# Attention scores from 50-row stacks of six bf16 products, with the heads in the two halves of TensorE's array

## The chip, the core and the metric

The kernel runs on one core of one Trainium2 chip. The metric is the device time of one launch in microseconds (us); lower is better.

## The reference

One layer: attention with a residual and a layer norm, then a mixture of experts with a residual and a layer norm. The input is 8 batches of 512 tokens with 128 channels. What matters here is the attention:

```python
qkv = x @ w_qkv + b_qkv
qkv = qkv.reshape(B, N_HEADS, S, 3 * HEAD_DIM)          # 8, 16, 512, 24: a head is 32 tokens wide in the buffer
q, k, v = jnp.split(qkv, 3, axis=-1)                    # HEAD_DIM = 8
scores = jnp.einsum('bhqd,bhkd->bhqk', q, k) * scale    # 512 x 512 for each of 128 (batch, head)
attn = jax.nn.softmax(scores, axis=-1)
vals = jnp.einsum('bhqk,bhkd->bhqd', attn, v)
```

Everything is float32. A float32 value is the sum of three bf16 parts (high, middle, low), so a score over 8 channels can be made as one bf16 matmul whose contraction rows hold products of parts: the kernel stacks part pairs over the partitions.

## The kernel before

The attention runs over 32 quads (a quad is 128 tokens of x and gives four heads of 512 queries and keys), four quads to a batch of the input. Each engine has its own program, ordered by hand, and goes through the same stages. Stage q does several things at once, for different quads:

- step `at` = 0 to 7 of the stage takes one half of one head. TensorE (PE) makes the plain scores of quad q + 2 (`score_a`, two matmuls of 512 columns into one of two pairs of PSUM banks), from which VectorE (DVE) takes the maximum over the keys (line 916). It also makes the transposed scores of quad q (`score_b`, two matmuls, one PSUM bank each), with the maximum subtracted by two more stack rows, and ScalarE (ACT) takes their exponential (line 883). The PE order inside a step is A, B, A, B.
- after each odd step PE multiplies the exponentials of quad q - 1 with v (`pvp`, line 1006): four float32 matmuls, one in each 32-column group.
- between steps there are jobs through one PSUM bank, `shared`: xT (the transpose of x, step 4), qkv (the projection, step 6), mT (the transpose of the maxima, step 1), valsT (the transpose of the output, step 3), and once a batch proj (i = 2, step 0), oT (i = 1, step 7), x1T (i = 3, step 5), gate (i = 3, step 7) and counts (i = 1, step 2). Here i is q modulo 4.

Two waits couple the engines inside a stage. The first matmul of `score_a` in a step waits for the maximum of two steps ago. A matmul of `score_b` waits for the exponential that last read its bank, the one of the same c in the step before.

The stacks are made as follows. After the qkv job of stage q - 1 (that is of quad q + 3) ACT copies q and k to SBUF, GpSimd (POOL) splits them into three bf16 parts (lines 810 to 816), SyncE's (SP) queue writes the parts to DRAM (line 742), waits for that write, and then reads them back as stack rows (lines 753 and 757). Stage q + 1 may begin on PE only when that stack is in. SP also loads x, the residual input (line 765), the experts' weights in stages 0 to 4, and stores the layer norm's output (line 644). POOL clears a buffer in DRAM in stages -1 to 7 (line 797) and later scatters rows into it.

In the kernel before a stack has 72 rows: nine products of parts by 8 channels (`KR = 9 * HD`), and 74 with the maximum's two rows. All four heads of a quad use the same partitions, one after the other in the free dimension.

Of the kernel before, what the change touches and what calls it, by code (L numbers as in the profile page):

```python
# [45 lines left out]
P = 128  # L46
# [58 lines left out]
def layer(nc, x, w_qkv, b_qkv, w_out, b_out, wg, ws1, ws3, ws2, we1, we3, we2, out):  # L105
# [26 lines left out]
    with ctx:  # L132
        def sb(name, shape, dt=F32):
            return ctx.enter_context(nc.sbuf_tensor(name, shape, dt))
# [8 lines left out]
        parts_dram = nc.dram_tensor("parts_dram", (2, 2, 4, 3, P, 32), BF16).ap()  # L143
# [143 lines left out]
        def need(eng, s, value):  # L287
# [4 lines left out]
            if not isinstance(value, int) and eng.engine in ALONE:  # L292


                eng.sem_inc(passed, 1)

# [398 lines left out]
        def attention_sync(sp):  # L695
# [36 lines left out]
            def stage(b, i):  # L732
# [3 lines left out]
                if has(b, i, 3):  # L736
# [5 lines left out]
                    sp.dma_start(parts_dram[par].rearrange("k h i p t -> p (k h i) t"),  # L742
                                 parts[:].rearrange("p k h i t -> p (k h i) t")).then_inc(parts_stored, 16)
# [34 lines left out]
        def attention_gpsimd(pool):  # L778
# [21 lines left out]
            def stage(b, i):  # L800
# [3 lines left out]
                if has(b, i, 4):  # L804
# [5 lines left out]
                    pool.tensor_copy(parts[:, :, :, 0, :], qk32[:]).then_inc(split_step, 1)  # L810
                    need(pool, split_step, 3 * n + 1)
                    pool.tensor_tensor(qkr[:], qk32[:], parts[:, :, :, 0, :], ALU.subtract).then_inc(split_step, 1)
                    need(pool, split_step, 3 * n + 2)
                    pool.tensor_copy(parts[:, :, :, 1, :], qkr[:]).then_inc(split_step, 1)
                    need(pool, split_step, 3 * n + 3)
                    pool.tensor_tensor(parts[:, :, :, 2, :], qkr[:], parts[:, :, :, 1, :], ALU.subtract) \
# [761 lines left out]
```

## Time and profile before

| | us |
|---|---|
| median of 3 runs | 738.19 |
| fastest, slowest | 734.01, 744.85 |
| the profiled execution | 739.75 |
| span of its instructions | 738.00 |

The profiled execution took 1.75 us more than the span from its first to its last instruction. Attention fills the trace up to about 515 us, and the mixture of experts the rest. The mean granted TensorE clock over the span is 0.964.

### The profile page before, as it was taken

The numbers are of one execution on the slowest core, as the hardware profiler recorded it, in microseconds if no ns is written. First come the engines' busy times: TensorE is split into PE (matmuls) and PEld (weight loads), VectorE is DVE, ScalarE is ACT, GpSimd is POOL, SyncE is SP. The second block draws the span as 40 slices with busy tenths as digits, with TensorE's granted clock in tenths as the row PEclk, the third lists the DMA queues.
The fourth block names the chain that finished last, engine by engine and source line by source line (L and its number), as shares of the span: only waits on it lengthen the run. The fifth ranks groups of instructions, "written<-read, shape, count | busy, mean of one in ns | idle before, by whom it ended". The sixth has DMA issues, their size and how long they took to land.

```text
span 738.0 us, 16592 instructions
## 1 busy us (share of the span) xinstructions
PE 657.1 (89%) x4593; PEld 315.6 (43%) x4594; DVE 551.3 (75%) x1272; ACT 426.0 (58%) x973; POOL 268.9 (36%) x402
## 2 busy tenths in 40 slices
PE   1899999999999999999999999997979898887880
PEld 1232333333333433433333343332568676666660
DVE  4967777879979969987996997974566566765763
ACT  1056677667766757666775666666342354454552
POOL 3124114213342244143434224306053265555553
PEclk9999999999999999999999999999899999999985
DMA  4366675543244233333233323302320333343322
GB/s 79 72 147 138 150 142 109 112 110 78 54 95 92 52 75 81 68 85 79 54 62 82 93 54 72 73 2 58 100 59 22 82 84 98 93 139 108 100 73 71
DMA packets 161854, 62.65 MB, mean 85 GB/s; under 512 B 110586, under 2 KB 155516, under 8 KB 161808
## 3 DMA queue, kind: packets, MB, share of 16 engines
q1 hardware_dynamic: 152960, 46.46, 29.0%
q0 software_dynamic: 5648, 13.26, 5.9%
q10 hardware_dynamic: 3200, 2.36, 1.0%
q8 instruction: 23, 0.38, 0.2%
q14 instruction: 23, 0.19, 0.1%
HBM read 38.04 MB, written 24.26 MB: 84 GB/s over the span
## 4 chain that ended last, share of the span: by engine, by line
PE 78%; ACT 5%; issue 5%; DVE 5%; DMA 2%; another core or an unknown queue 2%; POOL 1%; SPq 1%; ACTq 0%; DVEq 0%; POOLq 0%
PE pvp L1006 17%; PE scoreB L986 16%; PE scoreA L972 15%; PE scoreB L1520 5%; ACT prob L883 3%; PE pvp L1507 2%; PE scoreA L1497 2%; PE scoreA L1499 2%; PE scoreA L1498 2%; PE shared L525 2%; PE shared L514 2%; PE scoreB L1447 1%; DVE mx L916 1%; PE shared L544 1%
## 5 line engine op out<-in xcount | busy, mean ns | idle before, releaser
L916 DVE TENSOR_REDUCE mx<-scoreA 128x2 f32<-128x1024 f32 x256 | 306.3, 1220 | 77.0 <-PE scoreA L972 74.1
L883 ACT ACTIVATE prob<-scoreB 128x512 f32<-128x512 f32 x512 | 279.8, 600 | 128.0 <-PE scoreB L986 122.4
L972 PE MATMUL scoreA<-ks,qs 72*128 72x512 bf16 x512 | 205.7, 409 | 12.6 <-DMA ks<-parts_dram 10.2
L986 PE MATMUL scoreB<-qs,ks 74*128 74x512 bf16 x512 | 200.5, 394 | 15.3 <-ACT prob L883 11.9
L1006 PE MATMUL pvp<-prob,v 128*32 128x512 f32 x1024 | 141.4, 626 | 0.8 <-ACT pv_sb L875 0.8
L972 PEld LDWEIGHTS scoreA<-ks,qs 72*128 72x128 bf16 x512 | 51.0, 102 | 156.1 <-DVE mx L916 65.5
L986 PEld LDWEIGHTS scoreB<-qs,ks 74*128 74x128 bf16 x512 | 49.8, 98 | 110.6 <-ACT prob L883 85.3
L1166 POOL DMA_INDIRECT y_dram<-prob x72 | 70.6, 981 | 71.3 <-ACT prob L1397 43.3
L810 POOL CAST parts<-qk 128x256 bf16<-128x256 f32 x32 | 12.7, 396 | 227.9 <-ACT v_raw L563 208.6
L488 POOL DMA_INDIRECT slots_dram<-rows,slot_i x64 | 63.3, 990 | 31.7 <-issue 17.4
L1397 ACT ACTIVATE prob<-scoreB,prob 128x128 f32<-128x128 f32 x72 | 26.5, 368 | 38.4 <-PE scoreB L1520 26.1
L1520 PE MATMUL scoreB<-w,prob 128*128 x288 | 47.1, 289 | 0.0
L1336 DVE TENSOR_TENSOR prob<-scoreA,prob 128x256 f32<-128x256 f32 x72 | 30.4, 422 | 22.0 <-ACT prob L1390 16.2
L1390 ACT ACTIVATE prob<-scoreA 128x256 f32<-128x256 f32 x72 | 27.6, 383 | 28.1 <-PE scoreA L1499 17.9
L1497 PE MATMUL scoreA<-w_high,ebT_high 128*128 x72 | 35.7, 496 | 8.2 <-DVE ebT_low L1271 5.2
L1520 PEld LDWEIGHTS scoreB<-w,prob 128*128 128x128 f32 x288 | 40.1, 201 | 0.5
L1507 PE MATMUL pvp<-ident,prob 128*128 128x128 f32 x144 | 29.6, 288 | 11.0 <-DVE prob L1341 9.6
L1271 DVE TENSOR_TENSOR ebT_low<-scoreA,ebT_high 128x128 fp32r<-128x128 f32 x72 | 20.7, 288 | 23.5 <-ACT ebT_high L1365 15.9
L1006 PEld LDWEIGHTS pvp<-prob,v 128*32 128x32 f32 x1024 | 20.6, 109 | 31.0 <-issue 29.4
L1341 DVE COPY prob<-pvp 128x256 f32<-128x256 f32 x72 | 29.8, 414 | 2.0 <-remote 1.2
L559 ACT ACTIVATE qk<-shared,bq 128x128 f32<-128x128 f32 x64 | 20.0, 363 | 17.8 <-PE shared L514 12.0
L1507 PEld LDWEIGHTS pvp<-ident,prob 128*128 128x128 f32 x144 | 16.5, 145 | 30.6 <-issue 19.9
(172 smaller groups left out, 880.4 us busy)
## 6 DMA issues: line engine op xcount, KB each, us to landing
qs<-parts_dram SPq DMA_DIRECT2D x96, 96.0 KB
parts_dram<-parts SPq DMA_DIRECT2D x32, 192.0 KB
slots_dram<-blank POOLq DMA_DIRECT2D x9, 520.0 KB
prob<-slots_dram SPq DMA_DIRECT2D x72, 65.0 KB
ks<-parts_dram SPq DMA_DIRECT2D x64, 64.0 KB
prob<-y_dram SPq DMA_DIRECT2D x8, 512.0 KB
ks<-parts_dram SPq DMA_DIRECT2D x32, 96.0 KB
xin<-in_L_attn_x SPq DMA_DIRECT2D x32, 64.0 KB, 2.0
```

The costliest lines, as they stand in the source:

```text
L488: pool.indirect_dma_start(slots_dram, bass.IndirectOffsetOnAxis(ap=slot_i[:, j, t:t + 1], axis=0), rows[:, t, j, :], None).then_inc(scatte ...
L883: act.activation(prob[:, i % 2, j, 2 * u + c, :], scoreB[:, c], ACT.Exp, scale=SCALE).then_inc(exp_done, 1)
L916: dve.tensor_reduce(mx[:, i % 2, at // 2, at % 2 * 2:at % 2 * 2 + 2], scoreA[:, at % 2], AX.X, ALU.max).then_inc(max_done, 1)
L972: ins = pe.matmul(scoreA[:, at % 2, c], qs[0:KR, st, j, qc * P:(qc + 1) * P], ks[0:KR, st, j, :], start=True, stop=True)
L986: pe.matmul(scoreB[:, c], ks[0:KM, i, j, kc * P:(kc + 1) * P], qs[0:KM, i, j, :], start=True, stop=True).then_inc(b_ready, 1)
L1006: ins = pe.matmul(pvp[32 * h:32 * h + 32, :], v[:, (i - 1) % 2, h, j, :], prob[:, (i - 1) % 2, h, j, :], start=(j == 0), stop=(j == 3))
L1166: pool.indirect_dma_start(y2_dram, bass.IndirectOffsetOnAxis(ap=eb[:, at, D:D + 1].bitcast(I32), axis=0), yo[:, r, :], None, bounds_check= ...
L1336: dve.tensor_tensor(gated[:, r % 2, :], scoreA[:, 0, r % 2, F:2 * F], silu[:, r % 2, :], ALU.mult) \
L1341: dve.tensor_copy(gatedT[:, (r - 1) % 2, :], pvp[:, 0:F]).then_inc(gT_copied, 1)
L1497: pe.matmul(h, ebT_high[:, r % 2, 0:P], high, start=True, stop=False)
L1507: ins = pe.transpose(pvp[:, c * P:(c + 1) * P], gated[:, (r - 1) % 2, c * P:(c + 1) * P], ident[:])
L1520: ins = pe.matmul(y, gatedT[:, r % 2, c * P:(c + 1) * P], w2_flat[:, bass.ds(e * NFC * D + c * D, D)], start=(c == 0), stop=(c == NFC - 1))
```

## The change

The three smallest of the nine products are left out (middle times low, low times middle, low times low), so a stack has 48 rows, and 50 with the maximum's two. Heads 0 and 2 of a quad lie in partitions 0 to 49, heads 1 and 3 in partitions 64 to 113. The matmuls of both score loops become tiles of 64 rows by 128 columns at row 0 or at row 64 of the array. `score_b` takes the heads in the order 1, 0, 3, 2 (`head_b`), so that in each step A and B lie in different halves. The buffers `parts`, `qs` and `ks` are laid out to fit. The split's four POOL instructions keep their sizes. The stack is read back with 12 transfers instead of 8, which together move two thirds of the bytes (each row of 512 tokens is 1 KB).

```diff
-    KR = 9 * HD
-    PR = 3 * HD
-
-    K_ROWS = [(0, 0, 3), (PR, 1, 3), (PR + 2 * HD, 0, 1), (2 * PR, 2, 3), (2 * PR + HD, 0, 2)]
-    STACK_DMAS = 3 + len(K_ROWS)
+    KR = 6 * HD
     KM = KR + 2
+    HALF = P // 2
+
+    PRODUCTS = ((0, 0, 3), (3 * HD, 0, 2), (5 * HD, 0, 1))
+    STACK_DMAS = 4 * len(PRODUCTS)
...
-        parts = sb("parts", [P, 2, 4, 3, 32], BF16)
-        qs = sb("qs", [P, 4, 4, 512], BF16)
-        ks = sb("ks", [P, 4, 4, 512], BF16)
+
+        parts = sb("parts", [P, 4, 6, 32], BF16)
+
+        qs = sb("qs", [P, 4, 2, 512], BF16)
+        ks = sb("ks", [P, 4, 2, 512], BF16)
...
+        def head_b(at):
+
+            return at // 2 ^ 1
+
...
-                    for r in range(3):
-                        sp.dma_start(qs[PR * r:PR * (r + 1), st],
-                                     parts_dram[par, 0].rearrange("h i (d c) t -> (i d) h (c t)", d=HD)) \
-                          .then_inc(stack_loaded[par], 16)
-                    for row, i0, i1 in K_ROWS:
-                        sp.dma_start(ks[row:row + HD * (i1 - i0), st],
-                                     parts_dram[par, 1, :, i0:i1].rearrange("h i (d c) t -> (i d) h (c t)", d=HD)) \
-                          .then_inc(stack_loaded[par], 16)
+                    for row, first, end in PRODUCTS:
+                        for half in range(2):
+                            at = HALF * half + row
+                            n_rows = HD * (end - first)
+                            for to, s0 in ((qs, first), (ks, 6 - end)):
+                                sp.dma_start(to[at:at + n_rows, st],
+                                             parts_dram[par, half::2, s0:s0 + end - first]
+                                             .rearrange("h s (d c) t -> (s d) h (c t)", d=HD)) \
+                                  .then_inc(stack_loaded[par], 16)
...
-                                act.activation(prob[:, i % 2, j, 2 * u + c, :], scoreB[:, c], ACT.Exp,
+                                act.activation(prob[:, i % 2, head_b(2 * j), 2 * u + c, :], scoreB[:, c], ACT.Exp,
...
-                                act.dma_start(qs[KR + m:KR + m + 1, (i + 1) % 4].rearrange("p h x -> p (h x)"),
+                                act.dma_start(qs[KR + m::HALF, (i + 1) % 4].rearrange("p h x -> p (h x)"),
...
-            dve.memset(ks[64:96, 0], 1.0).then_inc(ones_set, 1)
+            dve.memset(ks[:, 0], 1.0).then_inc(ones_set, 1)
...
-                        ins = pe.matmul(scoreA[:, at % 2, c], qs[0:KR, st, j, qc * P:(qc + 1) * P],
-                                        ks[0:KR, st, j, :], start=True, stop=True)
+                        row = HALF * (j % 2)
+                        ins = pe.matmul(scoreA[:, at % 2, c], qs[row:row + KR, st, j // 2, qc * P:(qc + 1) * P],
+                                        ks[row:row + KR, st, j // 2, :], start=True, stop=True)
...
-                        j, kc = at // 2, at % 2 * 2 + c
+                        j, kc = head_b(at), at % 2 * 2 + c
...
-                        pe.matmul(scoreB[:, c], ks[0:KM, i, j, kc * P:(kc + 1) * P], qs[0:KM, i, j, :],
-                                  start=True, stop=True).then_inc(b_ready, 1)
+                        row = HALF * (j % 2)
+                        pe.matmul(scoreB[:, c], ks[row:row + KM, i, j // 2, kc * P:(kc + 1) * P],
+                                  qs[row:row + KM, i, j // 2, :], start=True, stop=True).then_inc(b_ready, 1)
```

The instructions of PE, ACT, DVE and POOL keep their order and number. The one queue whose contents change is SP's. In the loop over batches, in the stage i = 0, from the write of the parts to the end of the stack's loads, SP's queue before holds these rows (the two REGISTER_ALU rows belong to a wait):

```order
L742 DMA parts_dram<-parts 128x24x32
L291 REGISTER_ALU x2
L753 DMA qs<-parts_dram 24x4x512 x3
L757 DMA ks<-parts_dram 24x4x512
L757 DMA ks<-parts_dram 16x4x512
L757 DMA ks<-parts_dram 8x4x512 x2
L757 DMA ks<-parts_dram 16x4x512
```

In the changed kernel SP's queue holds these rows in the same place, of which four are left out ahead of the last four:

```order
L748 DMA parts_dram<-parts 128x24x32
L293 REGISTER_ALU x2
L763 DMA qs<-parts_dram 24x2x512
L763 DMA ks<-parts_dram 24x2x512
L763 DMA qs<-parts_dram 24x2x512
L763 DMA ks<-parts_dram 24x2x512
...
L763 DMA qs<-parts_dram 8x2x512
L763 DMA ks<-parts_dram 8x2x512
L763 DMA qs<-parts_dram 8x2x512
L763 DMA ks<-parts_dram 8x2x512
```

Nothing moved past anything else; the loads went from 8 to 12, and each covers two heads instead of four.

## Rows read from the trace of the kernel before

**Rows 1.** The page: busy time of each engine, and the chain that ended last.

```profile
PE 657.1 (89%) x4593; PEld 315.6 (43%) x4594; DVE 551.3 (75%) x1272; ACT 426.0 (58%) x973; POOL 268.9 (36%) x402
...
PE 78%; ACT 5%; issue 5%; DVE 5%; DMA 2%; another core or an unknown queue 2%; POOL 1%; SPq 1%; ACTq 0%; DVEq 0%; POOLq 0%
```

**Rows 2.** Windows (us, then PE, PEld, DVE, ACT, POOL, granted clock): stage 4, then stages 16 to 19.

```profile
98.78:112.41 13.63, 13.56 (x107) 4.74 (x106) 10.43 (x12) 9.91 (x22) 3.32 (x7) 1.00 0.73 146
...
277.23:292.00 14.77, 14.04 (x108) 4.76 (x106) 13.49 (x29) 10.61 (x23) 5.95 (x9) 1.00 0.42 94
292.00:306.41 14.41, 14.35 (x113) 5.67 (x114) 13.14 (x30) 9.92 (x22) 5.39 (x11) 1.00 0.30 60
306.41:321.10 14.69, 14.66 (x116) 5.68 (x114) 13.84 (x32) 10.23 (x22) 3.64 (x7) 1.00 0.31 59
321.10:338.85 17.75, 16.41 (x118) 6.39 (x118) 11.46 (x16) 10.36 (x24) 7.17 (x11) 0.90 0.35 78
```

**Rows 3.** Waits from 68 to 470 us: waiter, releaser, total us, times, longest.

```profile
ACT prob L883 <- PE scoreB L986: 104.0, 94, 2.7
...
DVE mx L916 <- PE scoreA L972: 55.4, 73, 2.8
```

**Rows 4.** Timeline, PE and ACT, steps 0 and 1 of a stage: start, us.

```profile
319.92 0.39 PE L972 MATMUL scoreA<-ks,qs 72*128 72x512 bf16 x1
320.14 0.38 PE L986 MATMUL scoreB<-qs,ks 74*128 74x512 bf16 x1
...
320.62 2.16 ACT L883 ACTIVATE prob<-scoreB 128x512 f32<-128x512 f32 x4
...
321.76 0.39 PE L986 MATMUL scoreB<-qs,ks 74*128 74x512 bf16 x1
...
322.19 1.06 PE L1006 MATMUL pvp<-prob,v 128*32 128x512 f32 x8
323.19 0.39 PE L972 MATMUL scoreA<-ks,qs 72*128 72x512 bf16 x1
```

**Rows 5.** Timeline, PE, steps 6 and 7 of the stage before that.

```profile
316.13 0.39 PE L972 MATMUL scoreA<-ks,qs 72*128 72x512 bf16 x1
...
317.02 0.38 PE L509 MATMUL shared<-xT,wq 128*128 128x128 f32 x2
...
318.61 0.38 PE L986 MATMUL scoreB<-qs,ks 74*128 74x512 bf16 x1
318.92 1.06 PE L1006 MATMUL pvp<-prob,v 128*32 128x512 f32 x8
```

**Rows 6.** Timeline, SP's queue: stores of the parts and loads of stacks, three stages.

```profile
35.18 1.83 SPq L757 DMA_DIRECT2D ks<-parts_dram  x5
...
112.96 0.38 SPq L742 DMA_DIRECT2D parts_dram<-parts  x1
119.73 1.15 SPq L753 DMA_DIRECT2D qs<-parts_dram  x3
...
322.31 0.38 SPq L742 DMA_DIRECT2D parts_dram<-parts  x1
326.27 1.15 SPq L753 DMA_DIRECT2D qs<-parts_dram  x3
327.46 1.85 SPq L757 DMA_DIRECT2D ks<-parts_dram  x5
```

**Rows 7.** Timeline, PE at the start: the first matmul of stage 0, two later ones.

```profile
39.47 0.61 PE L972 MATMUL scoreA<-ks,qs 72*128 72x512 bf16 x1 [0.36 <-DMA ks<-parts_dram]
...
57.63 0.63 PE L972 MATMUL scoreA<-ks,qs 72*128 72x512 bf16 x1
58.06 0.63 PE L986 MATMUL scoreB<-qs,ks 74*128 74x512 bf16 x1
```

**Rows 8.** Timeline, a pause of PE in a stage i = 3; windows, late attention.

```profile
329.30 0.39 PE L986 MATMUL scoreB<-qs,ks 74*128 74x512 bf16 x1 [1.19 <-ACT prob L883]
...
490.00:508.00 18.00, 14.76 (x112) 4.03 (x105) 11.88 (x43) 12.81 (x26) 7.50 (x9) 1.00 0.07 21
```

More of the change, by code:

```diff
@@ L140, in sem @@
             return ctx.enter_context(nc.semaphore(name))
-        parts_dram = nc.dram_tensor("parts_dram", (2, 2, 4, 3, P, 32), BF16).ap()
+        parts_dram = nc.dram_tensor("parts_dram", (2, 4, 6, P, 32), BF16).ap()
         x1_dram = nc.dram_tensor("x1_dram", (TILES * P, D), F32).ap()
@@ L741, in stage @@
                     need(sp, stack_loaded[par], 16 * STACK_DMAS * (2 * b + (i + 3) // 2))
-                    sp.dma_start(parts_dram[par].rearrange("k h i p t -> p (k h i) t"),
-                                 parts[:].rearrange("p k h i t -> p (k h i) t")).then_inc(parts_stored, 16)
+                    sp.dma_start(parts_dram[par].rearrange("h s p t -> p (h s) t"),
+                                 parts[:].rearrange("p h s t -> p (h s) t")).then_inc(parts_stored, 16)
                     need(sp, parts_stored, 16 * (n + 1))
@@ L809, in stage @@
                     need(pool, split_done, n)
-                    pool.tensor_copy(parts[:, :, :, 0, :], qk32[:]).then_inc(split_step, 1)
+                    high, mid, low = parts[:, :, 0::5], parts[:, :, 1:5:3], parts[:, :, 2:4]
+                    full, rest = (t[:].rearrange("p k h t -> p h k t") for t in (qk32, qkr))
+                    pool.tensor_copy(high, full).then_inc(split_step, 1)
                     need(pool, split_step, 3 * n + 1)
-                    pool.tensor_tensor(qkr[:], qk32[:], parts[:, :, :, 0, :], ALU.subtract).then_inc(split_step, 1)
+                    pool.tensor_tensor(rest, full, high, ALU.subtract).then_inc(split_step, 1)
                     need(pool, split_step, 3 * n + 2)
-                    pool.tensor_copy(parts[:, :, :, 1, :], qkr[:]).then_inc(split_step, 1)
+                    pool.tensor_copy(mid, rest).then_inc(split_step, 1)
                     need(pool, split_step, 3 * n + 3)
-                    pool.tensor_tensor(parts[:, :, :, 2, :], qkr[:], parts[:, :, :, 1, :], ALU.subtract) \
-                        .then_inc(split_done, 1)
+                    pool.tensor_tensor(low, rest, mid, ALU.subtract).then_inc(split_done, 1)
                 if isinstance(b, int) and q == -4:
@@ L915, in stage @@
                         dve.wait_ge(a_ready, 8 * (q + 2) + at + 1)
-                        dve.tensor_reduce(mx[:, i % 2, at // 2, at % 2 * 2:at % 2 * 2 + 2], scoreA[:, at % 2], AX.X,
+                        h = at // 2
+                        dve.tensor_reduce(mx[:, i % 2, h % 2 * 2 + h // 2, at % 2 * 2:at % 2 * 2 + 2], scoreA[:, at % 2], AX.X,
                                           ALU.max).then_inc(max_done, 1)
@@ L944, in attention_vector @@
             dve.memset(v[:], 0.0).then_inc(cleared, 1)
-            dve.memset(ks[64:96, 0], 1.0).then_inc(ones_set, 1)
-            dve.memset(ks[64:96, 1], 1.0).then_inc(ones_set, 1)
+            dve.memset(ks[:, 0], 1.0).then_inc(ones_set, 1)
+            dve.memset(ks[:, 1], 1.0).then_inc(ones_set, 1)
             dve.memset(half[:], -0.5).then_inc(cleared, 1)
@@ L950, in attention_vector @@
             dve.memset(blank[:], 0.0).then_inc(cleared, 1)
-            dve.memset(ks[64:96, 2], 1.0).then_inc(ones_set, 1)
-            dve.memset(ks[64:96, 3], 1.0).then_inc(ones_set, 1)
+            dve.memset(ks[:, 2], 1.0).then_inc(ones_set, 1)
+            dve.memset(ks[:, 3], 1.0).then_inc(ones_set, 1)
             dve.wait_ge(cleared, CLEARS)
```

## The prediction

> **What bounds the kernel now.** I read the page first: PE is busy 89% of the span and holds 78% of the chain that ended last [rows 1]. Nearly all of the change lies in the attention, so I went on to windows of one stage each [rows 2]. In a stage i = 0, 1 or 2 PE is busy for 14.04 to 14.66 us of 14.4 to 14.8, but DVE is right behind with 13.14 to 13.84. Only in i = 3 is DVE far below (11.46 of 17.75). The reader should see here that a faster PE can give back about 1 us in three stages of four. The waits say the same: from 68 to 470 us DVE waited 55.4 us for plain scores [rows 3], which is all that this stretch can give before DVE is the bound. ACT waited 104.0 us for transposed scores [rows 3], but not evenly, and for that I read a timeline of single instructions. In steps 0 and 1 [rows 4] ACT's four exponentials stand without a gap from 320.62 to 322.78, and the B matmul at 321.76 starts when the second of them ends. There the loop B matmul, exponential, B matmul sets the pace, and PE waits in it. In steps 6 and 7 [rows 5] the qkv job lies between the steps, nobody is waited for, and PE's own work is the length.
>
> **The matmuls.** A score matmul follows the last at 0.22 us (319.92 to 320.14 [rows 4]). After the change A and B of a step lie in separate halves. Can they stream side by side? The trace shows no row tiles, but it shows column tiles: the eight records of a `pvp` group, each of 512 columns, are through in 1.00 us (322.19 to 323.19 [rows 4]), 0.125 us each, where 0.22 each would be 1.76. So tiles in separate parts of the array do overlap here. The bounds for B behind A are 0 and 0.22 us; I take 0.05, nearer to side by side. In PE-bound places a pair then takes 0.22 instead of 0.44.
>
> The Trainium skill, "TensorE: Matmul & The Clock Gate", section "The mechanism", has matmuls in distinct row groups start about 4 ns apart. With 4 ns for my 0.05 the sum would be 2 to 3 us lower (seven pairs a stage, 0.046 us each, in the eight stages that DVE does not bound). The timeline of this kernel has no such pair to test it on.
>
> - Steps 6 and 7: the four scores of step 6 take 316.13 to 317.02, 0.89 us [rows 5], and those of step 7 the same. Each four become about 0.45, so -0.88 us a stage.
> - The other three pairs of steps are set by the ACT loop. There only the 0.22 us between A and the first B goes: B(0) starts 0.17 us earlier and all behind it does, -0.17 each, -0.51 a stage. The remaining time of such a pair (1.62 us from the first B to the fourth [rows 4], and 1.00 of `pvp`) stays.
> - Shapes now change between scores (64 rows) and the full-array jobs, where before both had all rows. From the last score to a `pvp` of another shape it is 0.31 us (318.61 to 318.92 [rows 5]) against the 0.22 of a score, so 0.09; with mT between, nothing. I take 0.1 for a new switch, 0 to 0.2. Per stage two lie on the path (into valsT, into qkv), so +0.2; those around xT fall into ACT's time. The four stages of a batch add seven more around proj, oT, x1T, gate and counts, half of them hidden, under 0.1 us a stage, which I leave out.
>
> The Trainium skill, "TensorEngine Tiling (Array Packing)", section "Key Properties", says that a change of tiling mode drains TensorE, while a change of tile does not. That rule speaks against this change, since every full-array job now stands between two modes. A drain as large as the tail of a matmul, 0.39 - 0.22 = 0.17 us by these rows, at each of some six new switches a stage would take back about 1 of the 1.4 us. The trace shows 0.09 us at one change of mode, from scores to `pvp`, and none at another.
>
> Net for PE and its loop: -0.88 - 0.51 + 0.2 = -1.2 us a stage; -1.4 with proj, which takes the pair 0, 1 out of the ACT loop.
>
> **DVE.** Nothing of DVE's changes. Its floor is its busy time plus gaps inside chains of dependent instructions: I take 0.3 us, 0.1 to 0.6. So one batch [rows 2] goes: i = 0 from 14.77 to 13.8 (DVE; PE's loop would allow 13.6), i = 1 from 14.41 to 13.45 (DVE), i = 2 from 14.69 to 14.15 (DVE), i = 3 from 17.75 to 16.15 (PE, with 0.4 more since part of it runs at half clock and its pairs save twice as much). Together 61.6 to 57.55, -4.1 us.
>
> **The stack's chain.** This is the cover to watch. SP issues 12 loads instead of 8. Eight took 326.27 to 329.31, 0.38 each [rows 6], so 12 take 4.6, +1.5 us. Fewer bytes (two thirds) do not help a queue that is bound by issue. The time from the qkv job (317.02 [rows 5]) to the store (322.31) is 5.3, the store and its wait 4.0, the loads 4.6. The landing after them takes 2.5 where it ended a wait (SP's last load issued by 37.01, PE released at 39.47 [rows 6, 7]), and I allow 1.8 to 2.5. That is 15.7 to 16.4 us, and it must fit into one stage plus the 2.5 us from the qkv job to the next stage's start. So no stage can be shorter than 13.2 to 13.9 us. In the loop DVE's floor is as long, so the price is nothing. In stages 2 to 5, where DVE is busy for 10.43 only and PE's loop alone would give 12.4 (stage 4 is 13.63 [rows 2], 2 and 3 the same), it takes the gain away. In stages 6, 7 and 9 the store took 6.8 to 7.3 us (112.96 to 119.73 [rows 6]; two more like it) and the gain is gone too.
>
> **The start.** Loads of the first stacks are serial: +1.5 us at stage -2 and +3.0 at stage 0 (12 loads twice on one chain). Stage 0 then runs at the 1.2 GHz level (0.43 us a score, 57.63 to 58.06 [rows 7]), PE-bound at 4 x 0.43 = 1.71 a step. Side by side it is the ACT loop's 0.63 (a score's own time there) + 0.54 (an exponential, 2.16 for four [rows 4]) + 0.1 = 1.27, and 8 x 0.44 = 3.5 can come back. Sum 0.
>
> **The sum.** Three full batches (12 to 23): 3 x -4.1 = -12.2. Batch 24 to 27, without half clock: -3.7. Stages 8 to 11: -3.0. Stages 2 to 7: -1.5. Stage 1: -1.2. Stages 28 and 29 (DVE-bound): -0.5. Stages 30 and 31 have B alone, in one half at a time: +0.3 of switches. Memsets of the ones: half the elements per partition, under the first stack's wait, 0. m's two transfers on ACT and POOL's split: same sizes, 0. The mixture of experts: 0. That makes -21.8, and 739.75 - 21.8 = 718 us. The profiled execution lies 1.6 us above the median 738.19. I give 718, the upper of the two readings.
>
> **Rivals.** A change under about 2% (723.4 to 753) is what a measurement of this kernel can hardly tell from none.
>
> - *The halves do not stream side by side* (0.15, slower). Decides: if B behind A stays at 0.22. The evidence against is the `pvp` group, which is in columns, not rows. Then nothing is gained, switches cost 0.4 us a stage over 30 stages (+12), the start keeps its +3 and stages 6, 7 and 9 get 1.5 each: 739.75 + 19.5 = 759, at least 745.
> - *The stack's chain becomes the bound everywhere* (0.22, within 2%). For: the floor of 13.2 to 13.9 lies at DVE's. Decides: if landing takes 3.5 instead of 2.5 us, or stores stretch to 7 us in more stages, then stages in the loop stay at 14.4 to 15 and only i = 3 gains: 7 x -1.6 = -11, 729.
> - *Half clock more often* (0.07, slower). A PE pause of 1.19 us [rows 8] stands in the stage i = 3 whose clock was 0.90 [rows 2]; against it, from 490 to 508 us PE was busy for 14.76 of 18.00 us at clock 1.00 [rows 8]. Such a stage costs 17.75 - 16.1 = 1.6 us. In every stage that is 30 x 1.6 = 48 on 718, 766; in every third 734.
> - *DVE's floor without gaps and i = 3 at 14* (0.12, faster). With 4 ns between A and B and i = 3's pause gone: 7 batches x -2.3 more, 702.
>
> The forecast itself, 710 to 726, has 0.44. The range takes in the chain and the better case: 702 to 742. Faster by over 2% (under 723.4): 0.52; within: 0.30; slower: 0.18.
>
> **What would show it.** Step 1 right: B's matmul starts under 0.1 us behind A, and score forms read 48*128 and 50*128. DVE right: in i = 0 to 2 waits of DVE for scoreA nearly vanish. Chain: PE's waits for ks<-parts_dram after 60 us show it as a bound. Switches: the time from the last score to L509's successor above 0.3 us. It is wrong if A and B stay 0.22 us apart, or if the clock falls below 0.95.

## The result and the profile after

The changed kernel took 759.10 us (median of 4 runs, 758.89 to 762.52) where the kernel before took 736.10 (median of 4, 733.91 to 744.85). The ratio is 1.032, 95% interval 1.027 to 1.037: it is slower. Where a kernel's executions spread by more than 1.5% (same_half, clear_twoq, after_b, clear_after_b, eight and filler below), its ratio leaves some of them out and its median none. The profiled execution took 758.97 us, its span is 757.2 and the mean granted clock 0.932; before it was 739.75, 738.0 and 0.964. The page:

```profile
span 757.2 us, 16720 instructions
PE 623.8 (82%) x4593; PEld 281.2 (37%) x4594; DVE 548.4 (72%) x1272; ACT 422.0 (56%) x973; POOL 268.9 (36%) x402
...
PE 45%; DVE 13%; issue 11%; DMA 10%; ACT 9%; SPq 6%; another core or an unknown queue 3%; POOL 1%; ACTq 1%; DVEq 0%; POOLq 0%
```

Against [rows 1] PE has 33.3 us less to do, and its share of the chain fell from 78% to 45%. DMA and SP's queue now hold 16% of the chain where they held 3%. So PE was relieved, and something else took over. The timeline of PE shows the first half of that, in steps 4 and 5 of a stage i = 0:

```profile
301.13 0.39 PE L982 MATMUL scoreA<-ks,qs 48*128 48x512 bf16 x1
301.13 0.39 PE L997 MATMUL scoreB<-qs,ks 50*128 50x512 bf16 x1
301.36 0.38 PE L982 MATMUL scoreA<-ks,qs 48*128 48x512 bf16 x1
301.36 0.38 PE L997 MATMUL scoreB<-qs,ks 50*128 50x512 bf16 x1
302.52 0.33 PE L509 MATMUL shared<-ident,xin 128*128 128x128 f32 x1 [0.78 <-DVE vals L596]
```

A and B start together, and the next pair 0.23 us later: two scores in the time of one [rows 4]. The last row shows where the time goes that this frees. PE reaches the xT job 0.78 us before DVE has read the job ahead of it out of the one `shared` bank, and waits.

Stages 16 to 19, as windows that begin with DVE's first maximum of a stage (us, then PE, PEld, DVE, ACT, POOL, granted clock), answer to [rows 2]:

```profile
294.84:310.06 15.22, 13.05 (x115) 4.06 (x116) 14.01 (x30) 11.78 (x26) 6.78 (x10) 1.00 0.38 78
310.06:325.04 14.98, 13.14 (x111) 4.55 (x111) 12.95 (x31) 8.63 (x19) 4.69 (x10) 0.89 0.24 44
325.04:339.60 14.56, 13.27 (x118) 4.70 (x118) 13.96 (x33) 11.04 (x25) 3.94 (x8) 1.00 0.25 46
339.60:356.59 16.99, 14.37 (x116) 5.14 (x116) 11.37 (x17) 9.52 (x21) 6.67 (x10) 0.90 0.33 70
```

Together they are 61.75 us, and 61.62 before. PE is busy for 53.83 of them instead of 59.46, and nothing came of it. The waits from 68 to 490 us say the same: DVE waited 69.5 us for plain scores, more than the 55.4 before [rows 3].

```profile
ACT prob L891 <- PE scoreB L997: 113.7, 101, 3.8
DVE mx L925 <- PE scoreA L982: 69.5, 63, 4.4
```

Where are the 19.2 us of span? I took from both traces the time at which DVE takes the first maximum of each stage. Stage 12, the first of the loop, began at 215.62 us before and begins at 232.77 now: 17.15 us are lost ahead of it. Stages 12 to 27 take 246.34 us instead of 244.94 (1.40 more), and the rest 0.7 more. So the loss lies in the early stages, and the loop only fails to gain. (The loop of the trace before holds three stretches at half clock, in i = 3. Two later traces of whole-array kernels on a chip as slow, before12 and full72, have none there and take 239.3 us for the same stages. Against those the changed loop is 7 us longer.) The queues of SP and POOL from 55 us on, in stages 0 to 2, show how, first of the changed kernel and then of the one before:

```profile
55.07 0.41 SPq L728 DMA_DIRECT2D w<-in_L_ffn_We  x1
...
56.20 0.37 SPq L748 DMA_DIRECT2D parts_dram<-parts  x1
66.97 0.32 SPq L763 DMA_DIRECT2D qs<-parts_dram  x1
...
73.65 1.03 SPq L748 DMA_DIRECT2D parts_dram<-parts  x1
84.66 0.32 SPq L763 DMA_DIRECT2D qs<-parts_dram  x1
...
55.68 0.88 POOL L804 DMA_DIRECT2D slots_dram<-blank  x1
...
73.78 0.39 PE L982 MATMUL scoreA<-ks,qs 48*128 48x512 bf16 x1 [4.06 <-DMA ks<-parts_dram]
```

```profile
56.77 0.37 SPq L742 DMA_DIRECT2D parts_dram<-parts  x1
60.85 1.17 SPq L753 DMA_DIRECT2D qs<-parts_dram  x3
...
57.09 0.88 POOL L797 DMA_DIRECT2D slots_dram<-blank  x1
```

Before, SP stored the parts at 56.77, POOL's clear of the slots (520 KB) was issued 0.32 us behind it, and SP's first load followed the store by 4.1 us. Now SP is busy for longer, with the loads of the stage before (until 54.32) and with the experts' weights, and its store comes 0.52 us behind the clear. From store to first load it is 10.8 us, and 11.0 for the next stack, where the clear (71.83) is again issued ahead of the store. The seven gaps ahead of stages 1 to 7 are 7.4, 10.8, 11.0, 7.8, 8.6, 7.3 and 7.8 us, where before five of them were about 4 and two 6.8 and 7.1. In the other five of the seven the clear is issued 0.3 to 1.2 us behind the store, as before, and the gap is long all the same. What differs there is the weights: for the stacks of stages 2 to 5 SP issues a large load of them 1.1 to 1.8 us ahead of the store, where before it was 5.3 to 7.9 us. Over all traces in which the clear isn't held back, this gap is 7.6 to 11.0 us in the 13 cases with such a load 1.1 to 2.0 us ahead of the store, and 3.8 to 6.7 us in the 13 with it more than 5 us ahead. PE then stands still for the loads (4.06 us in the row at 73.78). In all PE's matmuls waited 12.5 us for `ks<-parts_dram` from 68 to 234 us, six times; before (68 to 217 us) its weight loads alone waited for that, 1.7 us.

These waits cost more than their own length. Behind the three longest of them after 60 us, 4.06 us up to 73.78, 1.72 up to 105.29 and 2.79 up to 182.90, the granted clock falls to the lower level at 74.7, 105.4 and 183.9 us, for 10.2 us each time. Stage 2, which took 13.64 us before, shows it:

```profile
74.43:91.52 17.09, 15.52 (x108) 4.14 (x106) 10.60 (x13) 9.99 (x22) 2.24 (x5) 0.70 0.67 119
```

The second thing that is new is the half clock in a stage i = 1. It follows a pause of PE:

```profile
313.05 0.40 PE L500 MATMUL shared<-both,lower 128*128 128x32 f32 x2 [1.04 <-DVE m L604]
313.29 0.39 PE L501 MATMUL shared<-both,ones 128*128 128x32 f32 x2
313.61 0.61 PE L982 MATMUL scoreA<-ks,qs 48*128 48x512 bf16 x1
```

PE runs ahead of DVE up to the counts job, waits 1.04 us for DVE (the row names `m`, made from the transposed maxima in `shared`), and the next score takes 0.61 us instead of 0.39. Below 500 us the clock is halved in 64.8 us of the changed kernel's trace and in 10.2 of the one before.

### The profile page after: what moved, and what is told of

It reads as the page before. It is cut to its first block, busy times and chain, and to the rows that moved or that the text cites. A ratio compares the mean times of both kernels' runs of the same rounds, so it can differ in the third digit from the quotient of the medians.

```text
span 757.2 us, 16720 instructions
## 1 busy us (share of the span) xinstructions
PE 623.8 (82%) x4593; PEld 281.2 (37%) x4594; DVE 548.4 (72%) x1272; ACT 422.0 (56%) x973; POOL 268.9 (36%) x402
## 4 chain that ended last, share of the span: by engine, by line
PE 45%; DVE 13%; issue 11%; DMA 10%; ACT 9%; SPq 6%; another core or an unknown queue 3%; POOL 1%; ACTq 1%; DVEq 0%; POOLq 0%
PE pvp L1017 10%; DMA parts_dram<-parts 8%; DVE mx L925 7%; ACT prob L891 5%; PE scoreB L1531 5%; PE scoreA L982 5%; SPq L763 5%; PE scoreB L997 3%; PE scoreA L1508 2%; PE pvp L1518 2%; PE scoreA L1510 2%; PE shared L531 2%; PE scoreB L1458 2%; PE scoreA L1509 2%
## 5 line engine op out<-in xcount | busy, mean ns | idle before, releaser
L997 PE MATMUL scoreB<-qs,ks 50*128 50x512 bf16 x512 | 182.5, 411 | 30.5 <-ACT prob L891 23.2
L982 PE MATMUL scoreA<-ks,qs 48*128 48x512 bf16 x512 | 175.4, 423 | 31.6 <-DMA ks<-parts_dram 26.2
L1017 PE MATMUL pvp<-prob,v 128*32 128x512 f32 x1024 | 152.8, 673 | 0.8 <-ACT pv_sb L883 0.8
L982 PEld LDWEIGHTS scoreA<-ks,qs 48*128 48x128 bf16 x512 | 36.6, 97 | 169.3 <-DVE mx L925 68.1
L494 POOL DMA_INDIRECT slots_dram<-rows,slot_i x64 | 63.3, 989 | 33.2 <-issue 17.4
L997 PEld LDWEIGHTS scoreB<-qs,ks 50*128 50x128 bf16 x512 | 37.8, 95 | 100.1 <-ACT prob L891 92.2
L1531 PE MATMUL scoreB<-w,prob 128*128 x288 | 45.0, 280 | 0.0
L1531 PEld LDWEIGHTS scoreB<-w,prob 128*128 128x128 f32 x288 | 38.4, 194 | 0.3
L1510 PE MATMUL scoreA<-w_high,ebT_low 128*128 x72 | 28.6, 397 | 0.0
```

What stands on the lines that cost most here:

```text
L494: pool.indirect_dma_start(slots_dram, bass.IndirectOffsetOnAxis(ap=slot_i[:, j, t:t + 1], axis=0), rows[:, t, j, :], None).then_inc(scatte ...
L982: ins = pe.matmul(scoreA[:, at % 2, c], qs[row:row + KR, st, j // 2, qc * P:(qc + 1) * P], ks[row:row + KR, st, j // 2, :], start=True, st ...
L997: pe.matmul(scoreB[:, c], ks[row:row + KM, i, j // 2, kc * P:(kc + 1) * P], qs[row:row + KM, i, j // 2, :], start=True, stop=True).then_in ...
L1017: ins = pe.matmul(pvp[32 * h:32 * h + 32, :], v[:, (i - 1) % 2, h, j, :], prob[:, (i - 1) % 2, h, j, :], start=(j == 0), stop=(j == 3))
L1510: pe.matmul(h, ebT_low[:, r % 2, 0:P], high, start=False, stop=True).then_inc(h_ready, 1)
L1531: ins = pe.matmul(y, gatedT[:, r % 2, c * P:(c + 1) * P], w2_flat[:, bass.ds(e * NFC * D + c * D, D)], start=(c == 0), stop=(c == NFC - 1))
```

## The experiments

There were fourteen runs, in four sets. Besides its time each was read by the start of stage 12 (the early part), the length of stages 12 to 27 (the loop) and the time at half clock below 500 us. One fact is needed to read them: in the second and third set the kernel before took 692 to 693 us, in the first and fourth 736 to 738, and these are different chips. On the chip of the second and third set the pause once a batch in i = 3 [rows 8] and the half clock behind it are gone (clear_before's stages i = 3 in the loop are 14.91 us long), and what follows stage 29 takes some 217 us instead of 252. So ratios, and traces of one chip, are compared. A second fact bears on the start of stage 12. Every trace begins with scores at the lower clock level (0.61 us each; no granted clock is on record there, and a window prints 1.00), and the first rise to the upper level comes between 57.9 and 72.4 us: at 60.5 in the kernel before, 61.0 in the changed kernel, 67.8 in before12, 72.4 in full72 (and 118.4 in same_half, where two scores never share the time of one). In full72 stage 1 takes 20.4 us for it, and stage 12 starts at 220.86, 5.2 us later than before, with no wait for a stack that would explain it. A few us between single traces can be this alone.

**before12.** The kernel before with the same bytes in 12 loads instead of 8.

```diff
                     for r in range(3):
-                        sp.dma_start(qs[PR * r:PR * (r + 1), st], parts_dram[par, 0]...)
+                        for h in (0, 2):
+                            sp.dma_start(qs[PR * r:PR * (r + 1), st, h:h + 2], parts_dram[par, 0, h:h + 2]...)
```

(and the `ks` load of three parts' rows in two as well.)

> The kernel before (72 rows, one tile of the whole array, its own order of heads) with the same bytes of a stack loaded in 12 transfers instead of 8. Theory S, the stack's chain: the 12 issues are what cost in the changed kernel, above all before stage 12, where the delayed store falls behind the experts' weights or behind a clear of the slots and takes 7 to 11 us. Then this kernel loses most of the 17 us that the changed kernel lost before stage 12: 745 to 755. Rival C, half clock and the tiles themselves: the loss comes from the shape of the matmuls, and this kernel stays within 5 us of the kernel before, 733 to 742.

Measured: 746.11 us, ratio 1.014 (1.005 to 1.023). Stage 12 starts at 227.39, 11.8 us later than before, with gaps from store to load of 7.8, 8.4 and 7.5 us; the stages i = 1 and 2 of the loop are as before (14.41 and 14.69). Of the 11.8 us, 1.75 lie ahead of stage 0, 2.4 in stage 1, which runs at the lower clock level until 67.8 us, and 6.7 in stages 3 and 4: there PE waits 2.31 us for a stack, and the clock is halved from 105.3 us on for 10.2 us. So the four issues alone do part of what the change did, by the same wait and the same half clock, and cost the loop nothing. But the gaps ahead of stages 1 to 3 stay at 3.9 to 4.0 us, where the changed kernel has 7.4 to 11.0: there the weights still lie 5.9 and 8.8 us ahead of the store, and issues alone don't bring the long gaps.

**full72.** The six products, but on the whole array in the old order, with zeros up to 72 rows and six loads.

```diff
-    KR = 6 * HD
+    KR = 72
...
-    STACK_DMAS = 4 * len(PRODUCTS)
+    STACK_DMAS = 2 * len(PRODUCTS)
...
-        qs = sb("qs", [P, 4, 2, 512], BF16)
+        qs = sb("qs", [P, 4, 4, 512], BF16)
...
-                        row = HALF * (j % 2)
+                        row = 0
```

> Six products as in the changed kernel, but all heads on partitions 0 on, zero rows up to 72 so that the matmuls have the shape of before, the old order of heads, and 6 loads a stack. Theory S: the chain gets 0.8 us shorter than before and moves a third fewer bytes, so the time is that of before or a few us less, 728 to 738. Rival C says the same of the shape (no more half clock than before). If it is slower than before, the split or the layout of the parts costs something that neither theory has.

Measured: 735.20, ratio 0.996 (0.991 to 1.001). Fewer bytes and fewer loads are worth 1% at most, and by the interval perhaps nothing.

**same_half.** The changed kernel with B in A's half: no two scores can run beside each other.

```diff
-            return at // 2 ^ 1
+            return at // 2
```

> The changed kernel with the heads of B in the order of A, so that both matmuls of a step lie in the same half; stack, loads and tiles unchanged. If side by side is worth what the pairs' 0.05 us for 0.22 us suggest but the gain is swallowed by waits, this kernel is slower than the changed one by 5 to 15 us (764 to 775). If a less busy PE falls to half clock and that costs what the overlap gives, the two are equal within 4 us and this one shows a clock nearer to 0.96.

Measured: 830.75 (809.16 to 860.41), even the shortest execution far above the 764 to 775 that were expected. Windows of a stage i = 1 and a stage i = 2 at full clock, and one of 24 us at half clock:

```profile
334.61:349.44 14.83, 14.79 (x113) 5.44 (x113) 13.21 (x30) 9.99 (x22) 5.38 (x11) 1.00 0.24 45
349.44:364.86 15.42, 15.39 (x116) 5.65 (x115) 14.08 (x32) 10.31 (x22) 3.65 (x7) 1.00 0.23 43
303.00:327.00 24.00, 24.00 (x109) 7.79 (x101) 10.01 (x20) 9.41 (x19) 6.47 (x9) 0.51 0.29 65
```

PE is busy nearly throughout, so these lengths are its work. The same scores one after the other on the whole array took 14.41 and 14.69 [rows 2]. The difference is 0.42 and 0.73 us a stage. Single rows show where it comes from, here around the xT job:

```profile
341.39 0.38 PE L997 MATMUL scoreB<-qs,ks 50*128 50x512 bf16 x1
341.70 0.33 PE L509 MATMUL shared<-ident,xin 128*128 128x128 f32 x1
341.96 0.39 PE L982 MATMUL scoreA<-ks,qs 48*128 48x512 bf16 x1
```

From the last score to the job it is 0.31 us and from the job to the next score 0.26; in the kernel before the same two are 0.22 (327.40 to 327.62) and 0.11 (to 327.73). So a change between 64-row tiles and the whole array costs 0.09 to 0.15 us, with six to eight new ones a stage. The Trainium skill, "TensorEngine Tiling (Array Packing)", section "Key Properties", says that a change of tiling mode drains TensorE; this trace agrees. The last row was not expected: PE was busy for all of the 24.00 us, at a clock of 0.51. In this execution the loop took 286.7 us, where four times its undisturbed stages (14.87, 14.83, 15.42, 16.55 to 16.64) are 247: such stretches cost the other 40 us. What brought the clock down while PE was busy is open.

**clear_after.** The changed kernel, with POOL issuing the clear of the slots only when the stage's parts are stored.

```diff
                 if isinstance(b, int) and -1 <= q < SLOTS // 8 - 1:
+                    need(pool, parts_stored, 16 * (q + 5))
                     clear_slots(q + 1)
```

> The changed kernel, except that POOL issues each clear of the slots only after the parts of that stage are stored. Theory S: the store of the fourth stack takes 4 us instead of 7.4, the later ones are no longer pushed behind the experts' weights, and stages 1 to 9 give back 8 to 14 us: 745 to 751. Rival: if the early loss is PE at half clock (74.7 to 84.9 us and 105.4 to 115.6 us) and not the stores, the time stays within 3 us of 759.

Measured: 746.98, ratio 1.013 (1.006 to 1.021), 12 us less than the changed kernel. In its trace (of 740.27 us, the shortest of five executions) stage 12 starts at 216.09 instead of 232.77, and the gaps from store to load in stages 1 to 7 are 3.7 to 6.4 us:

```profile
55.04 0.37 SPq L748 DMA_DIRECT2D parts_dram<-parts  x1
61.42 0.32 SPq L763 DMA_DIRECT2D qs<-parts_dram  x1
```

The loop is as long as in the changed kernel (246.9 us). No stretch of 10.2 us at half clock is left. So with the clear out of the store's way 16.7 of the 17.15 us come back in this trace, by one line: the store's wait beside the clear's transfers, with the half clock that followed from it, was the early loss. The four kernels of the second set have this line too:

**clear_before**, the kernel before with it, as the control.

> The kernel before with nothing changed but the slots clear behind the parts' store, the control for the other runs with it. S: 8 loads leave slack in all stages but 8, 9 and 11, so 0 to 4 us less than the kernel before, 733-738 at 737.6. If the clear's transfers matter to the kernel before as much as to the changed one (12 us): 725-728.

Measured: ratio 1.001 (0.997 to 1.005). The kernel before has nothing to gain from it, although the gaps of 6.8 to 7.3 us shrink to 5.1 and less. Its chain has slack there; the changed kernel's has almost none.

**clear_full72**, full72 with it.

> Six products with zero rows up to 72 on the whole array in the old order, six loads, with the slots clear behind the parts' store. 735.2 without the clear moved. S (the small store waits behind the clear's transfers): stages 5 to 11, where the gap from store to first load was 6.8 to 7.3 instead of 4.0, give back 2 to 6 us: 729-733. If these waits are covered by PE and DVE there: 734-737.

Measured: ratio 1.000 (0.997 to 1.003). The forecast of the chain theory, 729 to 733 at 737.6 or 0.989 to 0.994, was wrong: these waits are covered there.

**clear_pad64**, clear_after with zeros in the unused rows of each half.

```diff
-    KM = KR + 2
+    KR = 62
+    KM = 64
```

(and memsets that fill all of `qs` with zeros, as in pad64 and eight below.)

> The changed kernel with the slots clear behind the parts' store, and the stacks' unused rows of each half filled with zeros (A matmuls read 62 rows instead of 48, B matmuls 64 instead of 50; the same columns, the same outputs). C (half clock comes with the few rows that a half's matmul works on): the 12 stretches and 44.4 us of half clock of the kernel without the zeros fall to 4 stretches or fewer, and the time to 738-743. S and H (chain and handshakes; rows are no matter): 745-751, stretches within 9 to 15.

Measured: ratio 0.999 (0.997 to 1.001), with 17.1 us at half clock below 500 us. This set was on the other chip, so the expected times don't apply, and the run is read against **clear_after_b** of the third set (below), the same without the zeros: 0.999 and 17.1 us too. The number of rows that a half's matmul works on is not what brings the half clock.

**clear_twoq**, clear_after with the six loads of `ks` issued by ACT in step 3.

```diff
+                        if j == 1 and u == 1 and has(b, i, 3):
+                            act.wait_ge(parts_stored, 16 * (q + 4))
+                            load_rows(act, (i + 3) % 4, (i + 3) % 2, ks)
```

> The changed kernel with the slots clear behind the parts' store, and the six loads of ks issued from ACT's queue in step 3 while SP issues the six of qs. S (after the clear, the stack's chain is still the bound of the loop's stages): the chain is shorter by half of 4.5 us of issue, the stages i = 0 to 2 fall from about 15.0 to 13.8-14.2, in all 747 - 20 = 725-733. C and H (half clock, DVE's floor with handshakes and switches bound the loop): only the early stages 2 to 7 gain, 3 to 6 us in all, 741-748. If ACT's issues sit before its exponentials and cost it 6 x 0.1 us and more a stage, 748-760.

Measured: 794.34 us, ratio 1.139 (1.132 to 1.146), far outside every expectation. First the timeline of ACT's queue, then a row of its waits from 212 to 440 us:

```profile
322.96 1.07 ACTq L904 DMA_DIRECT2D qs<-m  x2
324.14 2.13 ACTq L708 DMA_DIRECT2D ks<-parts_dram  x5
```

```profile
ACT prob L895 <- issue: 43.6, 13, 4.9
```

An issue takes ACT 0.4 us (2.13 for five), not the 0.1 that I had allowed, and ACT also waited for the store. Its exponentials stood for 1 to 5 us about once a stage (13 times in some 13 stages, 43.6 us), and the clock was halved in 136.5 us. The kernel tells nothing of the chain; it tells that ACT has no room for six issues.

The third set, all on one chip, repeats the two bases and takes the changed kernel apart once more.

**after_b**, the changed kernel itself.

> The changed kernel itself once more, as the base of this set, because the kernel before took 737 us on the chip of the first sets and 692 us on another. Ratios to the kernel before on the same chip count here. If the loss is tied to the pauses of the slower chip: 0.995 to 1.015. If it is not (the early stages' chain and the half clock are there on every chip): 1.02 to 1.04.

Measured: ratio 1.025 (1.019 to 1.031), but unclear: the five executions run from 697.00 to 712.45 us, 0.6 to 2.8% above the 692.74 of the kernel before, and the ratio is near the upper end of that. The trace, of the 697.00, has the same early loss in small: gaps of 7.2, 9.8 and 10.4 us ahead of stages 1 to 3, waits of 2.72 and 3.84 us for a stack, and half clock behind them. So that loss is not tied to the pause of the other chip, but its size in the total, and with it which of the two expectations holds, is not decided.

**clear_after_b**, the clear behind the store.

> The changed kernel with the slots clear behind the parts' store, on the chip of this set. S (early chain): 1.5 to 2.2% faster than the changed kernel beside it, as 746.98 stood to 759.1 (0.984). Against the kernel before: 1.00 to 1.015.

Measured: ratio 0.999 (0.995 to 1.004), the median 2.0% below that of after_b (693.80 to 708.22; the executions run from 687.82 to 704.60 and from 697.00 to 712.45). Stage 12 starts at 211.77, against 221.78 in after_b and 217.66 in clear_before; stages 12 to 27 take 231.77, 230.29 and 232.85 us. On this chip, without the pause in i = 3, the changed loop does gain, 2.6 us.

**pad64**, the zeros alone.

```diff
-    KM = KR + 2
+    KR = 62
+    KM = 64
```

> The changed kernel with only the zeros in the unused rows (62 and 64 rows a matmul instead of 48 and 50), the clear where the change has it. C (half clock depends on the rows of a half's matmul): fewer and shorter half clock stretches than the changed kernel beside it, half as many or less, and 1 to 1.5% faster than that. Rows no matter: within 0.5% of it and the same number of stretches within a quarter.

Measured: ratio 1.014 (1.009 to 1.019), but in the profiled execution it is 7.6 us longer than after_b, with 41.0 us at half clock against 37.5. Its executions (701.20 to 704.51) lie within those of after_b, so no difference is shown, and its 8 stretches against 7 speak for "rows no matter", as clear_pad64 does.

**eight**, the changed kernel with 8 loads of a stack: the third entry of `PRODUCTS` isn't loaded and its rows hold zeros. The expectation calls that the smallest correction; by the order of the parts in the buffer (high first for q, last for k) it is the product of the two high parts. The matmuls' shapes and the attention's schedule are the same either way; the experts get other tokens, so the early stages and the loop are what counts.

```diff
-    STACK_DMAS = 4 * len(PRODUCTS)
+    STACK_DMAS = 4 * 2
...
-                    for row, first, end in PRODUCTS:
+                    for row, first, end in PRODUCTS[:2]:
...
+            dve.memset(qs[:, 0], 0.0)
```

> The changed kernel with the loads of the sixth product left out (8 loads of a stack instead of 12, as many as the kernel before; the smallest correction is missing from the scores, the rows hold zeros, every matmul is as wide and deep as in the changed kernel). S (the chain of 12 loads is what the change lost by): 1.5 to 3% faster than the changed kernel beside it, 0.99 to 1.01 of the kernel before, with the early stages 4 to 12 as short as before. H and C (handshakes, mode switches, half clock in the loop): at most 1% faster than the changed kernel, stages 12 to 27 unchanged within 0.1 us each.

Measured: ratio 0.999 (0.994 to 1.004), the median 1.8% below that of after_b (695.49 to 708.22; the executions run from 685.75 to 700.42). Stage 12 starts at 210.00 instead of 221.78. Five of the seven gaps of stages 1 to 7 are still 7.1 to 9.0 us; with four issues fewer they cost less (PE's longest wait for a stack among them is 2.45 us instead of 3.84). Stages 12 to 27 take 232.46 us, none of it gained. This and clear_after_b show the two factors of one chain: take away either the four issues or the wait of the store, and stage 12 starts 10 to 12 us earlier and the ratio is back at 1.

The undisturbed loop is best read in after_b, stages 23 to 26:

```profile
381.45:395.27 13.82, 12.37 (x116) 4.73 (x116) 11.28 (x17) 9.53 (x21) 6.68 (x10) 1.00 0.39 82
395.27:410.00 14.73, 13.12 (x115) 3.97 (x115) 14.14 (x29) 11.56 (x26) 6.76 (x10) 1.00 0.37 83
410.00:423.69 13.69, 11.65 (x111) 4.22 (x110) 12.77 (x30) 8.64 (x19) 4.69 (x10) 1.00 0.28 51
423.69:438.25 14.56, 13.27 (x118) 4.68 (x118) 13.97 (x32) 11.04 (x25) 3.93 (x8) 1.00 0.24 46
```

These four take 56.80 us where the same four of clear_before take 58.21 (14.91, 14.20, 14.41 and 14.69). Of the 56.80 DVE is busy for 52.16, gaps under 0.15 us between its instructions are 1.40, and waits only 3.1. That is all that this change could still win here. The longest is this, at the end of i = 3:

```profile
392.64 1.06 PE L550 MATMUL shared<-w_g,valsT 128*128 128x8 f32 x8 [0.46 <-ACT v_raw L569]
393.63 1.07 PE L1017 MATMUL pvp<-prob,v 128*32 128x512 f32 x8
...
395.27 1.23 DVE L925 TENSOR_REDUCE mx<-scoreA 128x2 f32<-128x1024 f32 x1 [1.83 <-PE scoreA L982]
```

PE waits for ACT to read the qkv job, does gate and `pvp`, and only then makes the score that DVE has been out of for 1.83 us. The pair side by side saved 0.44 us in steps that were not the ones waited for.

**filler** and its base **clear_after_c**. What is left is whether PE's pause at the counts job brings the half clock of i = 1. In filler the last A matmul of that step is issued five times over, behind the last B, on the same data.

```diff
-                        ins = pe.matmul(scoreA[:, at % 2, c], ...)
+                        for again in range(5 if i == 1 and at == 2 and c == 1 else 1):
+                            ins = pe.matmul(scoreA[:, at % 2, c], ...)
...
-                    score_a(at, 1)
-                    score_b(at, 1)
+                    for score in (score_b, score_a) if i == 1 and at == 2 else (score_a, score_b):
+                        score(at, 1)
```

> The changed kernel with the slots clear behind the parts' store, as the base for the run with fillers. On the chip where the kernel before takes 692 us: 0.995 to 1.004 of it; where that takes 737: 1.008 to 1.02.

> The same with PE's pause of 1.04 us ahead of the counts job (once a batch, in step 2 of stage i = 1, behind which a pvp group of 1.06 us took 1.94 at half clock) filled: the last A matmul of that step is issued five times over instead of once, behind the last B. C (the pause brings the half clock): the stretches at 58 us intervals are gone, stage i = 1 is 13.7 instead of 14.8, 4 to 6 us less in all, a ratio of 0.992 to 0.994 to the run without fillers. If the half clock has another cause, the stretches stay and the time is within 0.3%, or up to 0.5% longer if DVE waits for the later scores.

Measured: 742.34 us and a ratio of 1.011 (1.007 to 1.015) without fillers, 740.79 and 1.003 (0.999 to 1.007) with them. 1.003/1.011 is 0.992, the expected size, but it isn't shown: the intervals of the two ratios touch, the medians differ by 0.2% only, and the executions overlap (738.90 to 748.76 without fillers, 732.33 to 746.86 with them). What filler shows lies in the stages. A stage i = 1 of each at about the same place, clear_after_c first:

```profile
418.46:433.58 15.12, 13.08 (x111) 4.56 (x111) 12.96 (x31) 8.63 (x19) 4.68 (x10) 0.89 0.24 44
```

```profile
293.51:307.22 13.71, 12.43 (x115) 4.51 (x114) 12.80 (x31) 8.64 (x19) 4.70 (x10) 1.00 0.26 48
```

With fillers three of the four stages i = 1 in the loop are 13.71 or 13.72 us long; without, three of four are 15.00 to 15.23. The same four stages in the eight traces of the changed kernel and its variants with this pause (after, clear_after, clear_after_c, after_b, clear_after_b, pad64, clear_pad64, eight) are 14.67 to 15.23 us long in 27 of 32 cases, and 13.69 or 13.92 in the other five. The pause is 1.04 us long in 31 of the 32; the one without it (0.05 us, in clear_after_c) is the 13.92. In filler 0.24 to 0.26 us of it are left. So more work for PE made these stages shorter. Without the long pause one stage of five is a long one, with it 27 of 31: the pause was the cause, in most cases and not in all. The gain is 1.3 to 1.5 us a stage, too little to be seen in the total. The stages i = 3 keep their pause and their half clock in both.

No kernel beat the kernel before by more than the measurement can tell. The best, full72, stands at 0.996 (0.991 to 1.001).

## Why the prediction was wrong

The forecast was 718 us, the range 702 to 742, and the measured 759 lies above it. By stretches of the profiled execution: stages up to 11 were to give back 5.7 us and lost 17.2; stages 12 to 27 were to give 15.9 and lost 1.4; the rest was to give 0.2 and lost 0.7.

- *The step that failed first is the stack's chain,* and in it the term "the store and its wait 4.0". The prediction calls the chain "the cover to watch", puts it at 15.7 to 16.4 us, and says that in stages 2 to 5 it "takes the gain away" and in the loop costs nothing. Of its terms the issues came out right (4.6 forecast, 4.7 to 6.2 measured), and the landing was shorter than the 1.8 to 2.5 taken: 1.3 to 1.5 us where PE waited for it. The store failed: it took 7.3 to 11.0 us in all seven stages where 4.0 was taken, so that wherever PE waited for a stack ahead of stages 1 to 9, 17.9 to 23.6 us passed from its qkv job to its first score. The prediction priced the chain as a gain not had. It added time instead, and it let PE stand still, which the prediction nowhere has, with three stretches of 10.2 us at half clock behind. A cover that is used up has no room for what before was hidden in it: SP now comes to its store right behind the weights and beside the clear. The 12 loads ahead of them are one reason; the other must be the faster stages, since eight, with 8 loads, has its store 1.1 to 2.0 us behind the weights too, and gaps of 8.7 to 9.0. I had read the 6.8 to 7.3 us gaps [rows 6] as a fixed feature of stages 6, 7 and 9, and not asked what lies beside them. before12 (+11.8 us ahead of stage 12, part of it by the clock's late first rise), clear_after and eight show both factors. The working also has 2.5 us from the qkv job to the next stage's start where its own rows give 2.9 (317.02 to 319.92 [rows 4, 5]); that would lower its floor by 0.4.
- *"Sum 0" for the start* was two estimates of 3 us and more set against each other. Stage 0 in fact began 0.8 us later than before and was 0.3 us shorter (15.3 against 15.6), so the sum was 0.5 and nearly right. What the terms would have been apart no run shows. Stage 1, at whose end PE waits 4.06 us behind the first gap of 11, grew from 14.9 to 17.4.
- *Side by side* was right, and better than assumed: 0.00 us from A to B instead of 0.05. The Trainium skill, "TensorE: Matmul & The Clock Gate", section "The mechanism", has 4 ns between the starts, and the rows at 301.13 agree within their 0.01.
- *Switches*: the price of one was right (0.1 taken, 0.09 to 0.15 by the rows of same_half). I counted two of them a stage on the path; where PE is the bound, as in same_half, all count, 0.4 to 0.7 us. The prediction's own sign for them, over 0.3 us from the last score to the job, came true with 0.31.
- *DVE's floor*, busy time plus 0.3 us, was right in the small gaps (1.40 us in four stages), but DVE doesn't reach it, and its waits for plain scores, which were to "nearly vanish", grew. It keeps waits of 3.1 us a batch, since PE's order is fixed and every job through `shared` waits for a reader. i = 0, 1, 2 came out at 14.73, 13.69 and 14.56 undisturbed, for a forecast of 13.8, 13.45 and 14.15; i = 3, which was to fall to 16.15, is at 16.99 in the changed kernel's trace. Part of that is also DVE's own time, 52.3 us in stages 16 to 19 instead of 51.9.
- *Half clock* was a rival at 0.07, with the pause of i = 3 as its only source. A new source came with the change: PE is now early at a job whose bank DVE has yet to read. It costs 1.0 to 1.5 us in most stages i = 1. And the waits for the stack bring the same in the early stages. The mean clock, 0.932, fell below the 0.95 that the prediction had named as a sign of being wrong. The price of 1.6 that the rival gave was of the right size, its chance too small.
- *The rival whose time was met, 759,* was the one in which the halves don't stream side by side. The time fits by luck: its mechanism is refuted by the first rows of the result. The rival "the chain becomes the bound everywhere" had the mechanism nearest to what happened, in the early stages alone, and priced it as gain lost, never as time added.

Open: what stops ACT and DVE together once a batch in i = 3 (2.6 us of ACT before, 3.2 after, 6.3 to 6.5 us behind SP's store in both traces) on the chips where the kernel takes 737 us, and why the clock falls behind it in the trace before but not in before12 and full72, which have the same pause. Also open is what keeps the undisturbed loop off DVE's floor: the waits for the readers of `shared` are read from rows, and no run moved a job.

## What to carry to other kernels

When a change makes the bounding engine faster, list the chains that ran beside it and ask of each how much slack it has left, and then what that slack was covering. Count a queue's issues, not its bytes. And an engine that becomes early in a fixed order waits at the next shared buffer; on TensorE such a pause can cost more than it lasts, by the clock behind it (here 1.0 to 1.5 us behind one of 1.04, in most cases). Before a start time in one trace is compared with another's, look when the clock first rose in each.

## What was not expected of the hardware

- TensorE at half clock while busy: in same_half it was busy for 24.00 of 24.00 us at a granted clock of 0.51, and for 41.00 of 41.00 at 0.50 from 453 us.
- A pause of 1.04 us was enough for a stretch at half clock behind it, and four score matmuls of 0.22 us each in its place kept the clock at 1.00, in three stages of four.
- A store of 192 KB took 4 us from issue to the first load that waited for it in most places, and 11 when it came 0.5 to 1.8 us behind a clear of 520 KB and 1.1 us behind a 1 MB load of weights. With the weights ahead and the clear held back it took 6.4.
- The first rise of the clock came at 57.9 us in eight and at 72.4 in full72, with PE at work from about 18 us in both.
- The same kernel took 692 us on one chip and 737 on two others. Of the 45 us some 35 lie behind the attention; the stages i = 3, with their pause, are 16.1 to 17.8 us long on the one and 14.91 on the other.
